# An fp32 to bf16 cast of streamed weights, moved from ScalarE to GpSimd, in a recurrent layer with a 17-expert FFN

## The reference

```python
u = xn @ B;  h[t] = sigmoid(A) * h[t-1] + u[t]          # scan over the tokens, 64 states
s = h @ C + xn @ D
mlp = lambda wg, wu, wd: (silu(xn @ wg) * (xn @ wu)) @ wd   # 1024 -> 512 -> 1024
r = sigmoid(xn @ gate_w + gate_b)                         # top 2 of 16, weights normed to sum 1
ffn = xn + mlp(shared) + sum over the two chosen experts of weight * mlp(expert)
out = x + s * silu(ffn)
```

## Time and profile before

| | us |
|---|---|
| time of two runs | 2083.86 and 2087.85, median 2085.86 |
| time of the profiled execution | 2091.2 |
| its span on the slowest core, core 1 | 2089.3 |
| spans of the eight cores | 2072.7 to 2089.3 |
| PE busy, of that span | 1619.7 (78%) |
| DVE busy | 831.5 (40%) |
| ACT busy | 372.5 (18%) |
| POOL busy | 28.0 (1%) |

### The profile page before, as it was taken

How to read it: one execution, slowest core, us unless ns; L and a number is a source line. 1 busy time by engine, 2 the same in 40 slices (tenths; PEclk the granted TensorE clock), 3 DMA queues, 4 the chain that set the end, 5 groups by cost and what they waited for, 6 DMA issues and landing times.

```text
span 2089.3 us, 18367 instructions; the slowest of 8 cores (2072.7 to 2089.3 us)
## 1 busy us (share of the span) xinstructions
PE 1619.7 (78%) x7074; PEld 690.3 (33%) x7074; DVE 831.5 (40%) x1662; ACT 372.5 (18%) x404; POOL 28.0 (1%) x32
## 2 busy tenths in 40 slices
PE   0133457897979788897979797979797979797997
PEld 0000123343434333333434343434343434342432
DVE  0277533343424243433334343424343424343442
ACT  0000011212121212122121212121212121212131
POOL 1000000000000000000000000000000000000012
PEclk9965687998989898999989898989898989898999
DMA  8812100203030302121211212121203030303048
GB/s 149 158 43 81 40 1 1 81 1 121 0 121 9 112 27 95 41 81 40 81 51 70 74 48 81 41 81 41 93 29 116 6 121 1 121 1 121 1 84 118
DMA packets 58872, 134.77 MB, mean 65 GB/s; under 512 B 3793, under 2 KB 8018, under 8 KB 57762
## 3 DMA queue, kind: packets, MB, share of 16 engines
q1 hardware_dynamic: 48354, 120.66, 17.7%
q0 software_dynamic: 10432, 12.95, 4.6%
HBM read 129.76 MB, written 16.78 MB: 70 GB/s over the span
## 4 chain that ended last, share of the span: by engine, by line
PE 68%; DMA 10%; DVE 7%; ACT 7%; issue 4%; another core or an unknown queue 4%; DVEq 1%; POOLq 0%; ACTq 0%; SPq 0%
PE pb L58 68%; DMA xt_buf<-ewu 7%; ACT warena L58 5%; DMA out<-inter_sb 2%; DVE acc L58 2%; DVE t_sb L58 1%; DVE x L58 1%; DVEq L70 1%; DVE inter_sb L58 1%; ACT silu_sb L58 1%; DVE xnT L58 0%; DMA xt_buf<-ewd 0%; DVE xb L58 0%; DVE rD L58 0%
## 5 line engine op out<-in xcount | busy, mean ns | idle before, releaser
L58 PE MATMUL pb<-xnT,warena 128*128 128x512 bf16 x4608 | 1064.5, 390 | 227.6 <-ACT warena L58 201.6
L58 PEld LDWEIGHTS pb<-xnT,warena 128*128 128x128 bf16 x4608 | 451.9, 100 | 806.9 <-issue 314.2
L58 DVE TENSOR_TENSOR t_sb<-silu_sb,pb 128x512 bf16<-128x512 bf16 x272 | 185.7, 688 | 948.1 <-ACT silu_sb L58 948.1
L58 PE MATMUL pb<-inter_sb,warena 128*128 128x512 bf16 x2176 | 491.4, 379 | 0.8 <-DVE acc L58 0.8
L58 DVE TENSOR_TENSOR acc<-acc,pb 128x512 f32<-128x512 f32 x576 | 367.4, 684 | 95.9 <-PE pb L58 95.5
L58 ACT ACTIVATE silu_sb<-pb 128x512 bf16<-128x512 f32 x272 | 160.6, 597 | 1065.7 <-PE pb L58 1065.6
L58 PEld LDWEIGHTS pb<-inter_sb,warena 128*128 128x128 bf16 x2176 | 212.7, 98 | 257.9 <-issue 2.9
L58 ACT ACTIVATE warena<-xt_buf 128x4096 bf16<-128x4096 f32 x49 | 177.2, 3616 | 278.8 <-DMA xt_buf<-ewu 138.2
L58 PE MATMUL pb<-xb,onesc 128*1 128x512 bf16 (+1 forms) x40 | 21.3, 533 | 99.3 <-DVE x L58 99.3
L58 DVE TENSOR_TENSOR inter_sb<-t_sb,m_sb 128x512 bf16<-128x512 bf16 x256 | 91.6, 420 | 5.9
L58 PE MATMUL pb<-xnT,bsb 128*64 128x512 bf16 (+1 forms) x40 | 16.3, 588 | 56.2 <-DVEq L58 56.2
(11 more groups left out here) (68 smaller groups left out, 249.8 us busy)
## 6 DMA issues: line engine op xcount, KB each, us to landing
xt_buf<-ewu SPq DMA_DIRECT2D x16, 2048.0 KB
xt_buf<-ewd SPq DMA_DIRECT2D x16, 2048.0 KB
xt_buf<-ewg SPq DMA_DIRECT2D x15, 2048.0 KB
out<-xt SPq DMA_DIRECT2D x1, 8192.0 KB
xt_buf<-xt SPq DMA_DIRECT2D x8, 1024.0 KB, 9.3
out<-inter_sb POOLq DMA_DIRECT2D x16, 512.0 KB, 7.0
xt_buf<-dmat SPq DMA_DIRECT2D x2, 2048.0 KB
xt_buf<-xt SPq DMA_DIRECT2D x2, 512.0 KB, 69.0
```

The costliest lines, as they stand in the source:

```text
L58: return Inst(getattr(self.real, name)(*a, **kw))
```

## The change

The cast in `wstage` is done by POOL in place of ACT: a `tensor_scalar_mul` by 1.0 with the same operands in place of an `activation` with Copy. The two waits in front of it (for the DMA, and for the slot) go to POOL with it, and it counts on the semaphore `s_gp` in place of `s_sc`. SP's DMA into `xt_buf` and the three places on PE that wait for a cast wait for `s_gp`.

```diff
                 if cast_last[0]:
-                    SY.wait(ssc, cast_last[0])
+                    SY.wait(sgp, cast_last[0])
...
-                SC.wait(sx, 16 * n_sx)
+                G.wait(sx, 16 * n_sx)
                 if retire_tkt:
-                    SC.wait(spe, retire_tkt)
-                kk = SC.op("activation",
-                           warena[:, slot * 4096:(slot + 1) * 4096],
-                           xt_buf[:, 0:4096], AF.Copy)
-                CAST_T[m] = kk.inc(ssc, 1)
+                    G.wait(spe, retire_tkt)
+                kk = G.op("tensor_scalar_mul",
+                          warena[:, slot * 4096:(slot + 1) * 4096],
+                          xt_buf[:, 0:4096], 1.0)
+                CAST_T[m] = kk.inc(sgp, 1)
...
-                        T.wait(ssc, CAST_T[m])
+                        T.wait(sgp, CAST_T[m])
...
-                            T.wait(ssc, CAST_T[m])
+                            T.wait(sgp, CAST_T[m])
...
-                        T.wait(ssc, CAST_T["D1"])
+                        T.wait(sgp, CAST_T["D1"])
```

## The result

The changed kernel takes 0.9172 of the time before, 95% interval 0.9157 to 0.9186: 8.3% faster. The profiled execution took 1916.0 us (span 1914.3, core 2) against 2091.2 before and 1839.2 forecast for it. The forecast of 1834 is missed by some 80 us, and the upper end of its range, 1895, by some 20. Seven of the eleven executions of the changed kernel, and one of ten of the kernel before, ran with a lower granted clock on one or both dies, and the medians of all are 1997.7 and 2088.5; ratios and times in this document leave such executions out, and a kernel that had no others is read on its undisturbed die.

A forecast was written before the change was run, and what follows sets the result against it. PE was bound by waits for ACT's casts, late in its queue, at changes of expert. 2091.2 - 262.0 + 7 + 3 = 1839.2 us for the profiled execution, 5.3 above the median, so 1834; range 1814 to 1895.

The forecast's parts named there:

- meetings of casts and products: In step tb = 1, POOL's cast of U holds the four products with `m_sb`; 7 us for 16 such casts.
- the second rival: Slower than before: the same meeting at a much longer cast; 2236 us at 15 us per cast; chance 0.04.
- 0.45 us of the sum: PE's loss per cast of U: products held 4.1 us, of which 3.65 us are covered.
- T: The last gate and up matmul of an expert, from which the forecast counts times of casts and transfers.
- The gain: All that the 16 changes of expert cost, 262.0 us, goes: 63 steps take 1331.8 us, not 1593.8.
- The hold: On DVE only the four products with `m_sb`, both operands from SBUF, wait for the rest of a POOL cast.
- e = 0: The cast of U of e = 1 falls among the router's small DVE instructions: 3 us lost.
- The tail: At the kernel's end, no gain: the last cast ended at 2005.0, PE came there at 2007.58 without it.
- slow casts that hold DVE: POOL casts of 6.5 to 10 us: 1874 us in all at 8, 1937 at 10.2; chance 0.24.
- Everything on DVE held (the fourth): Every DVE instruction is held by a cast: at most 264 us given back, about 2086 in all; chance 0.04.
- The clock (the third): Granted clock falls in the dense steps: 2167 us at 0.80, some 2140 by a 13/16 limiter; chance 0.04.

## Why the prediction was wrong, and where it was right

**The step that failed is one term of the sum: P, the length of a cast on POOL.** The forecast took 5.5 us between bounds of 2.29 and 10.2; it is 10.54, over the upper bound too, and the meetings of casts and products cost the steps 68 us where the sum had 7. The reason given, that nothing showed POOL to be faster than DVE's plain rate, guarded on the wrong side: nothing showed it not to be slower. The bounds came from other engines' rows. That is no bound on an engine whose time for an operation depends on the operation, 3.60 us for a copy and 10.54 for a product with a constant, in this case with the same operands.

**The mechanism was right, and its formula was near.** With the changed kernel's P the forecast's own working gives 16 x (10.54 - 5.05) = 88 us for U, 16 x (10.54 - 8.5) = 33 for D and, by the second rival's term, 16 x (21.08 + 9 - 26 - 3.65) = 7 for G. In all that is 1824 + 3 + 128 = 1955 on the median's scale, 1960 for the profiled execution. Measured were 1916. The excess is the tail of a cast: products are let go 1.88 us ahead of the recorded end. With 8.66 us for the hold, U costs 8.66 - 5.05 = 3.6 (3.67 read), D 0.2 (0.21 read) and G nothing.

**A second term stood at nothing: the clock behind such a gap.** A gap of 3.67 us can cost a second time, 14 us in all. Behind the 0.45 us of the sum there was little ground to expect it, but the first two rivals with their longer casts left it out too, though the prediction reads 1.66 us of slow matmuls behind each change of expert. The 68 us alone would have given 1824 + 3 + 68 = 1895, the very end of the range; the 14 carry the time out of it.

**One sum was wrong without harm.** The prediction says that PE waits for no cast unless P is near 40 us. In its own terms U is cast at T + 2P + 18 at the earliest and ready P later, and 3P + 18 reaches 88 at P = 23. The measured 10.54 is under both.

**The gain**, 262.0 us for 63 steps at 21.14, was right. The kernels without the meeting take 1332.1 (casts on ACT) and 1332.0 (copy) for these steps, against 1331.8. No cast was waited for by PE in any kernel with the casts in the free place.

**The page on GpSimd.** The Trainium skill, "GPSIMD Engine Reference", section 3.1, has 1.03 cycles per element for bodies of at most two operations. At the 1.2 GHz it gives, the copy took 1.05 cycles per column, which agrees, and the product by a constant 3.09, which does not. The 2.9 cycles, from which the prediction's 9.9 us come, stand in section 7 for reads with steps of over 8 bytes; the casts read fp32 in a row, so they are no upper bound for them.

**The hold** was as chosen: of DVE's work in the steps only the four products, which read both operands from SBUF, and for 8.66 of the 10.54 us. The rule of the Trainium skill in "SBUF — State Buffer", section "Who interferes with whom", that they exclude each other for a whole instruction, agrees with that but for the last 1.88 us, and with the products at 1.83 us once that instruction is short. At the end of e = 0 a copy from SBUF to SBUF on DVE was held as well (6.31 us beside the first cast of D, 0.69 otherwise), which the forecast did not have; it cost PE 1.2 us.

**e = 0**: 9 us lost for the 3 taken, for the same reason (P); that the steps began at the forecast 380.9 was luck, as said above. **The tail**: 1.3 us where the forecast had nothing.

**The rivals.** The first, slow casts that hold DVE, is what happened, with P just past its end of 10; its 1937 us for P = 10.2 are too many by the same tail. Everything on DVE held (the fourth) is out by the lengths of the other instructions. The much longer cast (the second) did not come. The clock (the third) did not fall over the dense stretches of the profiled execution, which had 0.99 over all 63 steps; it fell only behind idle time. That execution's clock records have no level but 0.50 and 1.00 on any of the eight cores, so the limiter at 13/16 that this rival names did not come in it.

## What to carry to other kernels

Ask of a stalled cast, copy or load first where it stands in its engine's program order, and whether a gap of its size exists elsewhere in the same engine's queue; here that kept the engine and won more than moving the work to another. An engine without a row for an operation has no price from other engines' rows: the range has to be wide above, or the operation is tried alone. Where GpSimd is given a cast like this one, a plain copy or a cut into pieces is the better form: the VectorE products with two SBUF operands stood still for most of one GpSimd instruction (8.66 of 10.54 us), and at most 0.84 us with pieces.

## What the runs showed of the hardware beyond this

- GpSimd, fp32 to bf16, 128 partitions: a tensor_scalar took 10.54 us for 4096 columns, 5.36 for 2048 and 2.77 for 1024, so some 2.53 ns per column and 0.18 us fixed. The copy took 3.60 us for 4096, 0.88 ns per column.
- When VectorE is let in beside a GpSimd tensor_scalar hangs on what waits. The products with two SBUF operands came in 1.9 us ahead of its recorded end, at 10.54 and at 5.36 us alike; a copy from SBUF to SBUF came in only 0.14 us ahead, at both lengths too. Beside a GpSimd copy the products came in 0.14 us ahead of its end. Why is not shown.
- Of sixteen idle times of PE of 3.67 us each on core 2, seven were followed by a stretch at the lower clock and nine were not; on the eight cores it was 5 to 7 of sixteen. What decides between them was not tried.
